# Perceiver kernel on one core: sort keys turned before the context products, the fourth count moved to ScalarE, and an ordering phase with a ring of 24 one-hot matrices

## The reference, cut to what matters

```python
q = _quantize(coords_bn3)                       # 10 bits per axis
qt = q[..., jnp.array([1, 0, 2])]
keys = [_morton_key(q), _morton_key(qt), _hilbert_key(q), _hilbert_key(qt)]
return [jnp.argsort(kk, axis=1) for kk in keys]
...
start = jnp.maximum(0, i - k // 2)              # window of ten places in the sorted order
```

## Time and profile before

| what | value |
|---|---|
| median of 3 runs | 1252.41 us (1238.13 to 1252.66) |
| profiled execution, its own time | 1249.17 us |
| span of the profile | 1247.5 us |
| mean granted TensorE clock | 0.885 |
| busy: PE, DVE, ACT, POOL | 961.2, 787.5, 443.7, 389.0 us |
| sort, from 14 us | to 176.5 us |
| ordering, stage 0 | 176.5 to 249.5 us |
| ordering, stage 1 | 394.0 to 472.2 us |

### The profile page before, as it was taken

One profiled execution on the slowest core, in us unless ns is written; L12 is line 12 of the kernel. 1 busy time (PEld: TensorE's weight loads), 2 busy tenths in 40 slices (PEclk: granted clock), 3 DMA queues, 4 the chain that ended last, 5 costly groups with the idle time before them and its releaser, 6 DMA issues. The chain is left out here.

```text
span 1247.5 us, 27210 instructions
## 1 busy us (share of the span) xinstructions
PE 961.2 (77%) x10400; PEld 681.3 (55%) x10400; DVE 787.5 (63%) x1896; ACT 443.7 (36%) x861; POOL 389.0 (31%) x302
## 2 busy tenths in 40 slices
PE   3791127687885887888955999994996699987798
PEld 2561114455563555666724999994642455553575
DVE  6859997678797766797954222337442459882642
ACT  0379314556333464542311222224000338780100
POOL 3000023399893337787702000000000055620000
PEclk9995558889897897899977999996998889998799
DMA  3744021222223154455502555541544527821000
GB/s 120 287 153 168 0 60 29 86 34 37 46 43 74 19 145 76 62 67 68 74 9 80 150 151 151 151 126 27 173 144 147 203 102 254 294 65 34 1 1 18
DMA packets 154876, 122.62 MB, mean 98 GB/s; under 512 B 52345, under 2 KB 129977, under 8 KB 153746
## 3 DMA queue, kind: packets, MB, share of 16 engines
q1 hardware_dynamic: 154402, 116.92, 35.5%
q10 hardware_dynamic: 368, 4.23, 0.8%
HBM read 108.79 MB, written 12.32 MB: 97 GB/s over the span
## 5 line engine op out<-in xcount | busy, mean ns | idle before, releaser
L569 POOL TENSOR_TENSOR stage_diff<-win_ext,win_F 128x960 f16<-128x960 f32 x88 | 161.8, 1840 | 21.5 <-PE attend_score L978 21.4
L725 DVE TENSOR_SCALAR order_place<-core_iota,points_rank 128x512 bf16<-128x512 f16 x256 | 92.1, 436 | 28.1 <-PE order_ordered L763 26.2
L1035 ACT ACTIVATE attend_prob<-attend_centred 124x480 f32<-124x480 f32 x88 | 52.3, 594 | 138.8 <-DVE attend_centred L1078 138.6
L763 PE MATMUL order_ordered<-order_place,order_piece 128*32 128x512 bf16 x768 | 77.3, 443 | 26.7 <-DVE order_place L725 14.9
L1273 DVE TENSOR_SCALAR attn_qT<-proj_qp,attn_bq,attn_gq 128x256 f32 x32 | 17.4, 544 | 122.7 <-ACT attn_sq L1252 122.7
L944 POOL TENSOR_TENSOR attend_pnorm<-attend_prob,attend_inv 124x480 f32<-124x480 f32 x88 | 86.8, 986 | 25.8 <-DVE attend_inv L1091 25.5
L1071 DVE TENSOR_REDUCE attend_top<-attend_score 124x32 f32<-124x480 f32 x88 | 56.0, 637 | 61.2 <-PE attend_score L978 61.0
L1006 PE MATMUL attend_outp<-stage_FX,stage_WX 128*64 128x240 f32 (+3 forms) x352 | 76.9, 398 | 8.8 <-DMA stage_vT<-scratch_values 8.8
L362 ACT ACTIVATE sort_signs<-sort_keysB,sort_key 128x512 bf16 x96 | 67.8, 713 | 14.5 <-DMA sort_keysB<-scratch_keys 14.1
L763 PEld LDWEIGHTS order_ordered<-order_place,order_piece 128*32 128x32 bf16 x768 | 38.2, 105 | 62.2 <-DVE order_place L725 17.5
L344 PE MATMUL sort_laterP<-sort_one,sort_equals 128*128 128x1 bf16 x192 | 14.5, 174 | 68.3 <-DVE sort_equals L473 68.3
(11 more groups left out here) (326 smaller groups left out, 2248.1 us busy)
## 6 DMA issues: line engine op xcount, KB each, us to landing
binary_base<-in_fmean_dram SPq DMA_DIRECT2D x8, 1344.0 KB, 9.5
cross_raw<-in_fw_dram SPq DMA_DIRECT2D x24, 448.0 KB, 7.5
stage_vT<-scratch_values SPq DMA_DIRECT2D x80, 120.0 KB, 5.4
sort_ctxT<-in_ctxT_dram SPq DMA_DIRECT2D x8, 1024.0 KB, 6.6
...
```

Of the source, the lines that this page charges most:

```text
L569: return nc.gpsimd.tensor_tensor(out[:, :, 0:size], spread, f.unsqueeze(3).to_broadcast([P, QB, size, WIN]), ALU.subtract)
L725: vec.tensor_scalar(place[n % RING][:], W["iota"][:], T["rank"][:, at:at + 1], None, ALU.is_equal).then_inc(place_ready, 1)
L763: mm = nc.tensor.matmul(ordered[b % 2][m * C:(m + 1) * C, :], piece[b // QB][:, k, t, r * C:(r + 1) * C], place[n % RING][:], start=(t == ...
```

## The change

In the sort:
- the six copies per axis order are made as 6 wider copies in place of 12;
- PE turns half 0 before the first context product, and half 1 before the last two contexts; ACT moves half 0 before its first evacuation; DVE copies half 0's turned keys a few instructions after the keys;
- ACT makes all four sign passes of a row, and DVE's `below` pass and its semaphore are gone;
- DVE marks the first two rows before it copies half 1's turned keys; `eq_used` is still primed after PE's last context product.

In the ordering:
- the ring has 24 place matrices, 16 of them in the memory of `hi[1]`, and the pieces lie in `lo4[1]`;
- batch 0 is multiplied piece by piece (all 16 places with piece 0, then piece 1, then piece 2), the other batches as before; the pieces of the second half are made between the first three `bring`s;
- the weights' loads are issued before SP waits for the features' store, and `combine` comes after batch 1, `shares` after batch 2;
- half of FX's rows come by 8 (stage 0) or 4 (stage 1) DMAs on SP's queue rather than by POOL's copy;
- the tail copy moves from POOL to ACT, `lo` of half 0 from POOL to DVE (after all places), and POOL starts differences and edges only when all 128 places are made; `scaled` runs one batch later.

```diff
-        signs = [s.sb(f"signs{u}", [P, N], BF16) for u in range(SIGNED)]
-        below = [s.sb(f"below{u}", [P, N], BF16) for u in range(2)]
+        signs = [s.sb(f"signs{u}", [P, N], BF16) for u in range(KC)]
...
+                turn_keys(0)
                 context.multiply_first(pe)
-                turn_keys(0)
-                context.multiply_others(pe)
+                context.multiply_others(pe, 0, B // 2 - 2)
                 turn_keys(1)
+                context.multiply_others(pe, B // 2 - 2, B // 2 - 1)
...
+                move_keys(act, 0)
                 for b in range(2):
                     context.evacuate(act, b)
-                move_keys(act, 0)
-
-                act.sem_inc(signed, SIGNED)
+
+                act.sem_inc(signed, KC)
 
                 def rows_of(m, first, count):
 
                     at = m * B + first
                     with act.Fori(0, count) as b:
-                        for t in range(SIGNED):
-                            act.wait_ge(signed, b * SIGNED + (at * SIGNED + t + 1))
+                        for t in range(KC):
...
-                for m in range(METHODS):
-                    for axis, c in enumerate((0, 1, 2) if m % 2 == 0 else (1, 0, 2)):
-                        go(vec.tensor_copy(S[:, axis, m, :], q[c]))
+                for m in range(2):
+                    for axis, c in enumerate((0, 1, 2) if m == 0 else (1, 0, 2)):
+                        go(vec.tensor_copy(S[:, axis, m:METHODS:2, :], q[c].unsqueeze(1).to_broadcast([P, METHODS // 2, BT])))
...
-                    if bit == NUM_BITS - 2:
-                        dve.wait_ge(turned, 1)
-                        vec.tensor_copy(keyT[0][:], keyP[0][:]).then_inc(keyT_ready, 1)
                     low_bits = (1 << bit) - 1
                     for a in range(3):
+                        if bit == NUM_BITS - 1 and a == 1:
+                            dve.wait_ge(turned, 1)
+                            vec.tensor_copy(keyT[0][:], keyP[0][:]).then_inc(keyT_ready, 1)
...
-                dve.sem_inc(counted, 2)
-                for m in range(METHODS):
-                    dve.wait_ge(keys_in[m], 16)
-                    with dve.Fori(0, B // 2) as pair:
+
+                def count_equals(m, first, end):
+                    with dve.Fori(first, end) as pair:
...
-                            dve.wait_ge(counted, pair * 2 + (m * B + u + 1))
-                            vec.tensor_scalar(below[u][:], keysB[:, bass.ds(pair * (2 * N) + (m * B + u) * N, N)],
-                                              keyF[:, bass.ds(pair * (2 * KC) + ((m * B + u) * KC + SIGNED), 1)], None, ALU.is_lt, ALU.add,
-                                              accum_out=order[:, bass.ds(pair * 2 + (m * B + u), 1), SIGNED]).then_inc(counted, 1)
+
+                dve.wait_ge(keys_in[0], 16)
+                count_equals(0, 0, 1)
+                dve.wait_ge(turned, 2)
+                vec.tensor_copy(keyT[1][:], keyP[1][:]).then_inc(keyT_ready, 1)
+                count_equals(0, 1, B // 2)
+                for m in range(1, METHODS):
+                    dve.wait_ge(keys_in[m], 16)
+                    count_equals(m, 0, B // 2)
                 dve.wait_ge(tied, METHODS * B * KC)
-                dve.wait_ge(signed, (METHODS * B + 1) * SIGNED)
+                dve.wait_ge(signed, (METHODS * B + 1) * KC)
...
-        piece = [s.sb(f"piece{t}", [P, 3, KC, P], BF16) for t in range(RT)]
+        lent = [W[k][1].rearrange("p r h n -> p (r h n)") for k in ("hi", "lo4")]
+        LENT = lent[0].shape[1] // N
+        piece = [lent[1][:, t * 3 * N:(t + 1) * 3 * N].bitcast(BF16).rearrange("p (k c n) -> p k c n", k=3, c=KC) for t in range(RT)]
         shared = s.sb("shared", [P, max(RT * 2 * N, B * EXT // 2)])
         rest = [shared[:, t * 2 * N:(t + 1) * 2 * N].rearrange("p (k c n) -> p k c n", k=2, c=KC) for t in range(RT)]
-        RING = 8
-        place = [s.sb(f"place{u}", [P, N], BF16) for u in range(RING)]
+        RING = LENT + 8
+        place = [lent[0][:, u * N:(u + 1) * N].bitcast(BF16) if u < LENT else s.sb(f"place{u}", [P, N], BF16)[:] for u in range(RING)]
...
+        def less_rows(sp, s2):
+            run = 1 if O == C else 2
+            from_batches = feat_d.rearrange("(q s a c n) -> s q c a n", s=2, a=run, c=C, n=N)[s2]
+            for q in range(KC // run):
+                sp.dma_start(FX[less(s2), q * run:(q + 1) * run, 0:N], from_batches[q]).then_inc(less_in, 16)
...
                 sp.dma_start(feat_d.rearrange("(t p n) -> p t n", p=P, n=N), T[src][:]).then_inc(feat_out, 16)
+                L.load(sp)
                 sp.wait_ge(feat_out, 16)
                 for m in range(METHODS):
                     sp.dma_start(F4[m * C:(m + 1) * C, :, 0:N], feat_d.rearrange("(b c n) -> c b n", c=C, n=N)).then_inc(feat_in, 16)
-                L.load(sp)
+                for s2 in range(2):
+                    less_rows(sp, s2)
...
+                remainders(0)
+                nc.gpsimd.memset(ext[:, :, 0:PAD], 0.0).then_inc(padded, 1)
                 nc.gpsimd.memset(WX[:], 0.0).then_inc(cleared, 1)
-                nc.gpsimd.memset(ext[:, :, 0:PAD], 0.0).then_inc(padded, 1)
                 nc.gpsimd.memset(F4[:, :, N:NP], 0.0)
                 go(nc.gpsimd.memset(FX[:, :, N:NP], 0.0))
+                remainders(1)
...
-                for s2 in range(2):
-                    go(nc.gpsimd.tensor_copy(FXs[less(s2), ..., 0:N], pairs[less(s2), s2, ..., 0:N]))
-
-                def end_of(q):
-                    pool.wait_ge(order_out, (q + 1) * QB)
-                    nc.gpsimd.tensor_copy(ext[:, half(q), PAD + N:EXT],
-                                          ext[:, half(q), PAD + N - 1:PAD + N].to_broadcast([P, QB, EXT - PAD - N])).then_inc(padded, 1)
-                    pool.wait_ge(padded, q + 2)
...
-                end_of(0)
-                pool.wait_ge(high_made, 1)
-                nc.gpsimd.tensor_tensor(W["lo"][:, half(0)], ext[:, half(0)], high[:, half(0)], ALU.subtract).then_inc(low_made, 1)
+                pool.wait_ge(place_ready, B * MT)
+                pool.wait_ge(padded, 2)
                 go(differences(nc, W, W["diff"][0], 0, 0, SB))
                 edges(0)
                 nc.gpsimd.tensor_copy(W["diff"][0][:, :, 0:PAD, :], W["edge"][:, 0:QB])
-                end_of(1)
+                pool.wait_ge(padded, 3)
...
-                    if b == 1:
+                    if b == 2:
                         shares()
-                    if b == B - 2:
-                        dve.wait_ge(low_made, 1)
-                        for h in range(HEADS):
-                            vec.tensor_scalar(lo[:, :, h, :], W["lo"][:, half(0), :], T["headmask"][:, h:h + 1], None, ALU.mult)
+                dve.wait_ge(high_made, 1)
+                vec.tensor_tensor(W["lo"][:, half(0)], ext[:, half(0)], high[:, half(0)], ALU.subtract).then_inc(low_made, 1)
+                dve.wait_ge(low_made, 1)
+                for h in range(HEADS):
+                    vec.tensor_scalar(lo[:, :, h, :], W["lo"][:, half(0), :], T["headmask"][:, h:h + 1], None, ALU.mult)
                 dve.wait_ge(high_made, 2)
-                dve.wait_ge(padded, 3)
                 vec.tensor_tensor(W["lo"][:, half(1)], ext[:, half(1)], high[:, half(1)], ALU.subtract)
...
+                def order_one(b, t, m, ks):
+                    n, r = b * MT + t * METHODS + m, b % QB
+                    for k in ks:
+                        mm = nc.tensor.matmul(ordered[b % 2][m * C:(m + 1) * C, :], piece[b // QB][:, k, t, r * C:(r + 1) * C],
+                                              place[n % RING], start=(t == 0 and k == 0), stop=(t == KC - 1 and k == 2))
+                    if ks[-1] == 2:
+                        mm.then_inc(place_used, 1)
+
+                def order_first():
+                    for k in range(3):
+                        pe.wait_ge(piece_ready, k + 1)
+                        for t in range(KC):
+                            for m in range(METHODS):
+                                pe.wait_ge(place_ready, t * METHODS + m + 1)
+                                order_one(0, t, m, (k,))
+
                 def order(b):
                     pe.wait_ge(piece_ready, (b // QB + 1) * 3)
                     if b >= 2:
                         pe.wait_ge(order_out, b - 1)
-                    r = b % QB
                     for t in range(KC):
                         for m in range(METHODS):
-                            n = b * MT + t * METHODS + m
-                            pe.wait_ge(place_ready, n + 1)
-                            for k in range(3):
-                                mm = nc.tensor.matmul(ordered[b % 2][m * C:(m + 1) * C, :], piece[b // QB][:, k, t, r * C:(r + 1) * C],
-                                                      place[n % RING][:], start=(t == 0 and k == 0), stop=(t == KC - 1 and k == 2))
-                            mm.then_inc(place_used, 1)
```

(37 more changed lines are left out.)

40 lines of the change are left out of this document (16 added, 24 removed).

## The result

The changed kernel takes 1189.17 us (median of 4 runs, 1187.90 to 1192.64), the kernel before 1252.54 (4 runs, 1238.13 to 1253.10): ratio 0.9525, 95% interval 0.9453 to 0.9596 (the ratio goes by all runs; that of the two medians is 0.949). One execution of experiment 12's kernel, the profiled one, took 1821.94 us against 1181.81 to 1184.75 for its other four, and is left out there. The profiled execution took 1190.31 us with a span of 1188.6, against 1249.17 and 1247.5.

A forecast was written before the change was run, and what follows sets the result against it. VectorE was taken to bound the sort, no single engine the ordering. Sort -20.0, stage 0 -16.6 and stage 1 -14.0 took 1249.17 to 1198.6 us profiled; 3.24 under the median, hence 1202, range 1190 to 1217.

The forecast's parts named there:

- Sort's mechanism: Sort: VectorE sets the end; with the fourth count on ScalarE a row takes 1.90 us, ordering starts at 156.5, gain 20.0.
- the hand-over: Sort: VectorE waits for PE's priming behind the last context, PE ending at 93.7 and VectorE's wait at 93.9.
- ScalarE's stall on the second keys: Sort, row 16: keys wanted at 106.0 arrive at 108.5, a stall of 2.5 us; ScalarE ends at 153.8, before VectorE.
- PE's batch: Ordering, both stages: a batch of 48 products takes about 3.5 us at full clock, from 46 products in 3.67.
- The tail of stage 0: Ordering, stage 0, behind the last batch: 9.1 us before, 0.7 more taken, so 9.8; 0 if hidden, 5 if wholly serial.
- `combine`'s wait: Ordering, stage 0: PE's 4.84 us wait for weights goes, since loads leave some 5 us earlier and `combine` comes a batch later.
- POOL's move: Ordering tail, stage 0: work moved to ScalarE and VectorE, POOL's differences and edges later; 0.7 us more, between 0 and 5.
- Rival 1: Sort: PE's contexts starve behind early keys, 7.5 us instead of 1.5, or second keys land late; 1208 us, chance 0.10.
- Rival 2: Ordering: VectorE's longer run of places keeps POOL's remainders out, 4 to 8 us a stage, 12 in all; 1214, chance 0.08.
- Rival 3: Ordering: places in lent memory are made at half VectorE's rate, 22.5 us a stage, 45 in all; 1247, chance 0.03.
- Rival 4: Sort and ordering: PE stays at its low clock after the idle start, sort +36 us; 1280, chance 0.02.
- Rival 5: More gain than forecast: no DMA stall, batches at 3.5 us throughout, no clash at the end; 1190, chance 0.10.

The follow-up runs named there:

- experiment 12: Changed kernel with marks primed early and eight buffer sets, last eight rows' fourth count on VectorE, second half's edges on VectorE: 1184.3 us, ratio 0.9501 to the kernel before.
- experiment 3: Changed kernel with the fourth tile's count back on VectorE, ScalarE making three passes: 1207.50 us, ordering starts at 175.97.
- experiment 5: Changed kernel with PE priming `eq_used` first in its queue, ahead of all contexts: 1189.5 us, ordering starts at 152.92.
- experiment 7: Changed kernel with a ring of 8 and batch 0 multiplied place by place, all three pieces at once: 1200.1 us, stages 62.52 and 67.28.
- Experiment 11: Changed kernel with the second half's window edges on VectorE instead of POOL: 1193.45 us, stage 0 at 53.98 with a tail of 11.0.

## Why the prediction was right, point by point

The forecast was 1202 us and the result 1189.2: the side and the mechanisms held, and the time came out 0.8 us under the range's lower end (by the ratio, 0.9525 of 1252.4, it would be 1192.9, inside it). Of the 12.8 us, 8.3 lie between the sum and the profiled execution, and 4.4 in the profiled execution's place: it lay 3.2 us under the median before and lies 1.1 above it now.

- **Sort's mechanism held.** The count's move is all of its gain (experiment 3), a row takes 1.90, the new order on VectorE frees nothing because of the priming (experiment 5). PE's end of 93.7 was met (93.68), with the third context's stall at 1.78 where 1.5 was taken. The term that was off is the hand-over: VectorE's first mark was put 0.2 us after PE's last product, and it came 1.8 before (91.86), since the sequencer's increment does not wait for the array. That is 2.0, of which the tail behind the last mark took a little back. The order of before has the same hand-over hidden, so no row showed it.
- **ScalarE's stall on the second keys was over-sized:** 2.5 taken, none seen. It was off the path and cost nothing.
- **PE's batch was the mis-sized term of both stages.** 3.5 us came from 46 products in 3.67; a burst of 48 takes 2.79 (190.84), 0.7 less a batch even with the last product's length in it. The granted clock is 1.00 in both (windows view of before, then of after, over each burst):
```profile
229.50:233.00 3.50, 3.50 (x52) 1.95 (x52) 2.70 (x9) 2.54 (x2) 0.00 (x0) 1.00 0.53 157
```
```profile
190.84:193.60 2.76, 2.76 (x51) 1.65 (x51) 2.76 (x12) 2.71 (x3) 0.00 (x0) 1.00 0.54 192
```
  So the row of before was not PE's rate but that of a ring of 8: with it, experiment 7 has the row of before again (46 products in 3.66), and with 24 in the same code 48 take 2.79. The sum fits as well: eight stored places at 3 x 0.05 and eight at VectorE's 0.27 are 3.3, and the row is 3.67 less the last product's 0.4. PE thus catches up with VectorE behind each pair of value products, and the last batch comes at 42.5 and 47.2 instead of 46.5 and 51.0. VectorE's own end was put at 43.2 and is at 41.2.
- **The tail of stage 0 was mis-sized the other way:** 9.8 taken, 13.1 measured. The bound "if wholly serial, 5" was the right end: POOL and VectorE did not work beside each other but took turns (edges of 0.58 instead of 0.23 us, one of 2.23 behind L754). Experiment 11 shows the share that the edges have. The two errors nearly cancel in stage 0 (55.6 against 56.3) and not in stage 1, where the tail is PE's: 61.3 against 64.1.
- **What the terms stood for.** `combine`'s wait was priced at 4.84 and a later row; undone, it costs 12 to 15 us, because with this order VectorE waits too and POOL is shut out behind it. POOL's move was priced as a matter of the tail, 0.7 to 5 us of loss; undone, it costs 7 to 8 us a stage. The parts' worth (7 for the ring, 12 to 15 for the weights, 7 to 8 for POOL) adds up to more than the 17 us gained: each removes a stop that is enough by itself to hold the stage back.
- **Rival 1** (contexts starve) did not come, at 1.78 us. **Rival 2** (POOL starves) is real but elsewhere: the first remainders go through at once, the third stands 5.97 us in stage 0 and 5.93 in stage 1, and the pieces it makes are first needed in batch 4. The Trainium skill (SBUF — State Buffer, Who interferes with whom) has VectorE in a two-port mode and GpSimd exclude each other, whichever issued first, for its whole instruction; the traces agree for the remainders of 1.2 us, beside which one place lasts about as long, and show that the waiting one can be passed over for a whole run of instructions (up to 11.51 us) or get in after one. So the prediction read its own row too kindly in "the trace agrees for both lengths": the copy of 4.75 us stood through 17 places, not through one. **Rival 3** (lent places slow): places in `stage_hi` and in `order_place` both take 0.27. **Rival 4** (low clock): the granted clock in the orderings is 0.93 and 0.95, before 0.85. **Rival 5** (more than forecast) named 1190, close to what came, but not for its reasons: of its three conditions only the batches held, and they were faster still than its 3.5; the DMA stall and the clash at the end came all the same.
- **Attention 1** was left alone in the forecast and gave 3.8 us. Its instructions are the same, the clock rises sooner (windows of 8 us, each starting some 8 us into the phase, before and after):
```profile
480.00:488.00 8.00, 8.00 (x144) 5.86 (x144) 3.74 (x8) 1.75 (x3) 6.12 (x5) 0.66 0.18 20
```
```profile
425.00:433.00 8.00, 8.00 (x181) 6.00 (x180) 4.16 (x9) 3.03 (x5) 7.43 (x7) 0.86 0.22 23
```
The mean of 0.66 against 0.86 lies between the two levels of 1.2 and 2.4 GHz. Over all kernels this phase took 194.9 to 202.3 us, by the chip rather than by the edit, so it is not counted as the change's gain.
